# Projecting a part's groups at once and reading x1 four groups behind, in a two-layer graph kernel

## What is computed

```
W         = einsum('rb,bio->rio', w_comp, weight)             # 16 types from 8 bases
node_repr = segment_sum((x @ W[type])[src], dst) + h_bias
x1        = layernorm(x + node_repr)
deg       = maximum(segment_sum(1, dst), 1)
agg       = segment_sum(x1[src], dst)
out       = layernorm(x1 + x1 @ W_self + b_self + agg / deg @ W_neigh)
```

## Time and profile before

| | us |
|---|---|
| median of 3 runs | 3176.4 |
| fastest, slowest run | 3176.38, 3180.55 |
| profiled execution, span | 4143.4 |
| span less median | 967.0 |

### The profile page before, as it was taken

One profiled execution on the slowest core, in us unless ns is written; L12 is line 12 of the kernel. 1 busy time (PEld: TensorE's weight loads), 2 busy tenths in 40 slices (PEclk: granted clock), 3 DMA queues, 4 the chain that ended last, 5 costly groups with the idle time before them and its releaser, 6 DMA issues. The chain is left out here.

```text
span 4143.4 us, 36092 instructions
## 1 busy us (share of the span) xinstructions
PE 2142.2 (52%) x12511; PEld 2001.1 (48%) x12511; DVE 1431.9 (35%) x3693; ACT 332.1 (8%) x668; POOL 2392.4 (58%) x2524
## 2 busy tenths in 40 slices
PE   2455555555655555465555555567144444444445
PEld 1455445555555555455555555566143333333345
DVE  5242222122221222222221221222255657666635
ACT  1110000000000000000000000001000000000001
POOL 6645555555555555555556555565666666666663
PEclk7776666666666666666666665666555666666666
DMA  3832332233332332333333332332112222122222
GB/s 103 240 104 83 93 89 84 83 89 93 87 89 85 93 87 83 87 88 89 87 87 93 88 86 85 87 98 70 47 53 54 54 54 61 53 61 62 61 81 64
DMA packets 257427, 345.24 MB, mean 83 GB/s; under 512 B 47008, under 2 KB 189957, under 8 KB 257238
## 3 DMA queue, kind: packets, MB, share of 16 engines
q0 software_dynamic: 104400, 263.16, 22.7%
q1 hardware_dynamic: 127398, 66.86, 5.5%
q10 hardware_dynamic: 25440, 12.85, 1.0%
HBM read 311.14 MB, written 44.38 MB: 86 GB/s over the span
## 5 line engine op out<-in xcount | busy, mean ns | idle before, releaser
L1639 POOL DMA_INDIRECT rows<-x_x_rows,src_t x1501 | 1427.7, 951 | 1164.2 <-DMA x_x_rows<-xout 463.0
L2241 PE MATMUL zps<-acc,rows 128*128 128x168 f32 x3322 | 761.6, 363 | 570.6 <-issue 461.1
L2241 PEld LDWEIGHTS zps<-acc,rows 128*128 128x128 f32 x3322 | 611.5, 226 | 644.3 <-issue 598.7
L1666 POOL DMA_INDIRECT rows<-x_rows,picked_mem x691 | 655.9, 949 | 347.0 <-issue 196.1
L1887 DVE TENSOR_TENSOR acc<-acc,yps 128x63 f32 (+1 forms) x563 | 123.6, 220 | 1162.2 <-PE yps L2276 966.5
L2255 PEld LDWEIGHTS yps<-oh,rows 128*128 128x128 f32 x2058 | 336.6, 229 | 315.6 <-issue 315.4
L2255 PE MATMUL yps<-oh,rows 128*128 128x21 f32 x2058 | 313.6, 275 | 323.4 <-issue 321.5
L1865 DVE TENSOR_TENSOR acc<-oh,tps 128x1344 f32<-128x1344 f32 x208 | 323.3, 1554 | 141.7 <-remote 108.2
L2376 PE MATMUL zps<-acc,rows 128*128 128x128 f32 x1382 | 274.3, 356 | 121.9 <-issue 117.0
L2376 PEld LDWEIGHTS zps<-acc,rows 128*128 128x128 f32 x1382 | 244.9, 263 | 144.3 <-issue 144.2
L1718 ACT COPY acc<-zps 128x672 f32<-128x672 f32 x208 | 148.2, 714 | 1977.8 <-remote 1786.4
(11 more groups left out here) (315 smaller groups left out, 1882.0 us busy)
## 6 DMA issues: line engine op xcount, KB each, us to landing
rows<-x_x_rows,src_t POOLq DMA_INDIRECT x1501
acc<-in_edge_type_dram SPq DMA_DIRECT2D x207, 64.0 KB
x_x_rows<-zrow ACTq DMA_DIRECT2D x20, 576.0 KB, 3.3
x_x_rows<-in_x_dram SPq DMA_DIRECT2D x20, 576.0 KB
rows<-x_rows,picked_mem POOLq DMA_INDIRECT x691
x_rows<-xout SPq DMA_DIRECT2D x49, 128.0 KB
xin<-in_x_dram SPq DMA_DIRECT2D x48, 128.0 KB
out_dram<-xout SPq DMA_DIRECT2D x24, 256.0 KB
```

What stands on the lines that cost most here:

```text
L1639: gather = pool.indirect_dma_start(out=wide_rows[:, g % WIDE_SLOTS, c, :], out_offset=None, in_=table, in_offset=bass.IndirectOffsetOnAxis ...
L1666: pool.indirect_dma_start(out=rows[:, j % SLOTS, c, :], out_offset=None, in_=x1_rows[0:n_nodes, :], in_offset=bass.IndirectOffsetOnAxis(ap ...
L2241: last = nc.tensor.matmul(zwins[g % 2][:, c // HALF, c % HALF // 2], slot_rows(g, c), a[:, g % 4, c], start=(c % 2 == 0), stop=(c % 2 == 1 ...
```

## The change

The groups of a part are no longer projected in pairs. `project(r)` (line 2297 of the changed kernel) multiplies all 4 or 5 groups of a part at once, with 336 or 420 columns, into a PSUM bank of its own (`tps[1]`), between the two halves of the next group; the first and the last part are split in two runs. `zsb` has room for 5 groups. DVE adds the layer sums of all of the part's groups one after the other in that round (`add_sums`), and the early sums and degrees of each pair apart from them (`add_pair_windows`), from two banks that take turns. The part is staged one group after its last one and turned in the group after that. READABLE is 8, and a part is first read at half group 2 * done_at(k) + 8, which is group done_at(k) + 4: four whole groups, 32 gathers, lie between. SP waits for the pair adds before it stores degrees. The constants that follow from `front` change a little: 859 late columns instead of 852. The steps of the preamble that work out the same numbers for the data are adapted, and a few tiles lie elsewhere.

```diff
-READABLE = 9
+READABLE = 8
+RUN = 5
...
-        return per_group * (max(h - READABLE, 0) // 4 * 2 + 1)
+        return per_group * (max(h - READABLE, 2) // 2 - 1)
 
     def front(h):
         return 0 if h < 2 * PLAIN else min(FRONT, readable(h) // 17)
...
-        sums = first_layer(4 * DUOS * n_bases * SPAN)
-        zsb = sums.rearrange("p (u w b n) -> p u w b n", u=4, w=DUOS, b=n_bases)
+        sums = first_layer(RUN * DUOS * n_bases * SPAN)
...
+            runs = []
+            for k in range(all_parts):
+                g0, g1 = done_at(k - 1) if k else 0, done_at(k)
+                middle = [2] if k == 0 else [last_group] if k == last_part else []
+                bounds = [g0] + middle + [g1]
+                runs += [(r0, r1, k, r0 == g0) for r0, r1 in zip(bounds[:-1], bounds[1:])]
+            run_of = {g: r for r, (r0, r1, k, first) in enumerate(runs) for g in range(r0, r1)}
+            run_ends = {r1: r for r, (r0, r1, k, first) in enumerate(runs)}
+            assert len(run_of) == groups and all(r1 - r0 <= RUN for r0, r1, k, first in runs)
+
+            staged_at = {done_at(k): k for k in range(all_parts)}
+            turned_at = {done_at(k) + 1: k for k in range(all_parts)}
...
+            cleared_at = {done_at(k) + 3: k for k in range(all_parts)}
...
-            loops_at = {(1, 3, 7, 11)[k]: k for k in range(len(quads))}
+            loops_at = {(2, 3, 4, 8)[k]: k for k in range(len(quads))}
...
-            banks = [ybank[0], ybank[1], tps[1][:, :, :].rearrange("p t e -> p (t e)")]
...
+            ybank1 = tps[1][:, :, :].rearrange("p t e -> p (t e)")
+            windows = [y[:, 0:2 * 2 * DUOS * SPAN].rearrange("p (k w n) -> p k w n", k=2, w=2 * DUOS) for y in ybank]
+
+            def sums_col(g):
+                r0, r1, k, first = runs[run_of[g]]
+                return (g - (done_at(k - 1) if k else 0)) * DUOS * SPAN
...
                         if k < last_part:
+                            sp.wait_ge(pair_added, done_at(k))
                             store_degrees(stored1[s])
...
-                            after(act, w1.y_done, g // 2 - 1)
-                            nc.scalar.copy(zsb[:, g % 4].rearrange("p (h w) b n -> p h (w b n)", h=2),
+                            after(act, w1.y_done, run_of[g])
+                            nc.scalar.copy(zsb[:, kept_at(g)].rearrange("p (h w) b n -> p h (w b n)", h=2),
                                            zduos[g % 2]).then_inc(w1.z_copied, 1)
...
-                    def add_sums(g):
-
-                        first = 1 if narrow(g) else 0
+                    def starts_of(g):
                         _, starts = nc.values_load_multi_w_load_instructions(
                             base[0:1, g * DUOS:g * DUOS + duos_of(g)], engines=DVE_ONLY, min_val=0, max_val=n_nodes,
                             skip_runtime_bounds_check_because="clamped to the number of nodes, and acc is padded")
-                        dve.wait_ge(w1.y_done, products_before(g))
+                        return starts
+
+                    def add_pair_windows(g):
+
+                        first = 1 if narrow(g) else 0
+                        starts = starts_of(g)
+                        dve.wait_ge(deg_done, g // 2 + 1)
+                        after(dve, pair_added, g)
+                        for c in range(duos_of(g)):
+                            target = kinds3[:, 2 * first:3:2, bass.ds(starts[c], SPAN)]
+                            if c:
+                                dve.wait_ge(pair_step, g * (DUOS - 1) + c)
+                            add = nc.vector.tensor_tensor(target, target, windows_of(g)[:, first:2, c, :], ALU.add)
+                            add.then_inc(pair_step if c < duos_of(g) - 1 else pair_added, 1)
...
+                    def add_sums(g):
+
+                        starts = starts_of(g)
+                        dve.wait_ge(w1.y_done, run_of[g] + 1)
                         after(dve, w1.group_added, g)
                         for c in range(duos_of(g)):
-                            target = kinds3[:, first:3, bass.ds(starts[c], SPAN)]
+                            target = mem[:, bass.ds(starts[c] + SHIFT, SPAN)]
+                            y0 = sums_col(g) + c * SPAN
                             if c:
                                 dve.wait_ge(w1.rmw, g * (DUOS - 1) + c)
-                            add = nc.vector.tensor_tensor(target, target, windows_of(g)[:, first:3, c, :],
-                                                          ALU.add)
+                            add = nc.vector.tensor_tensor(target, target, ybank1[:, y0:y0 + SPAN], ALU.add)
...
-                        if g % 2 == 0 and 2 <= g < groups:
-                            add_sums(g - 2)
-                            add_sums(g - 1)
-                        if groups <= g < groups + 2:
-                            add_sums(g - 2)
+                        if g % 2 == 0 and 2 <= g <= groups:
+                            add_pair_windows(g - 2)
+                            add_pair_windows(g - 1)
+                        if g in run_ends:
+                            for e in range(*runs[run_ends[g]][0:2]):
+                                add_sums(e)
                         if g in out_at:
                             part_done(out_at[g])
...
+                            last = nc.tensor.transpose(tps[1][:, j, :], stage[:, j, :], ident[:, :])
...
-                                bank_free("pair", g // 2)
-                            if g == last_group:
-                                bank_free("single", g)
+                                after(pe, pair_added, g - 2)
...
-                    def project_pair(p):
-                        pe.wait_ge(w1.z_copied, 2 * p + 2)
-                        two = zsb[:, 2 * p % 4:2 * p % 4 + 2].rearrange("p u w b n -> p (u w) b n")
+                    def project(r):
+
+                        r0, r1, k, first = runs[r]
+                        pe.wait_ge(w1.z_copied, r1)
+                        if first:
+                            after(pe, n1.added, k)
+                        else:
+                            pe.wait_ge(w1.group_added, r0)
+                        if r == 1:
+                            pe.wait_ge(s_loopc, len(quads) - 1)
+                        if r == 2:
+                            pe.wait_ge(s_loopc, len(quads))
+                        duos = (r1 - r0) * DUOS if r1 < groups else (last_group - r0) * DUOS + duos_of(last_group)
+                        kept = zsb[:, 0:r1 - r0].rearrange("p u w b n -> p (u w) b n")
+                        y0 = sums_col(r0)
                         for b in range(n_bases):
-                            last = nc.tensor.matmul(windows[p][:, 1], wb[:, b, :], two[:, :, b, :],
+                            last = nc.tensor.matmul(ybank1[:, y0:y0 + duos * SPAN].rearrange("p (w n) -> p w n", n=SPAN),
+                                                    wb[:, b, :], kept[:, 0:duos, b, :],
                                                     start=(b == 0), stop=(b == n_bases - 1))
                         last.then_inc(w1.y_done, 1)
...
                     scale_by_relation(0)
-                    for g in range(groups - 2):
+                    for g in range(groups):
...
                         sum_half(g, 0)
                         early_half(g, 0)
+                        if g in run_ends:
+                            project(run_ends[g])
                         if g in turned_at:
                             turn_part(turned_at[g])
                         sum_half(g, 1)
                         early_half(g, 1)
                         if g % 2:
                             count_pair(g // 2)
-                            project_pair(g // 2)
                         if g in loops_at:
                             turn_loops(loops_at[g])
-
...
+                    project(run_ends[groups])
                     turn_part(last_part)
```

115 lines of the change are left out of this document (38 added, 77 removed).

## The result

The changed kernel takes 3222.7 us (median of 4 runs, 3211.5 to 3227.5) where the kernel before takes 3176.4 (4 runs, 3176.0 to 3180.6): ratio 1.0141, 95% interval 1.0128 to 1.0153. That is 46.4 us slower. The forecast was 3185.1; the range, 3120 to 3225, holds the result near its upper end, because it was drawn to take in rival B, the slower one.

The account below looks back on a forecast made before the run. POOL's gathers were taken to bound both phases, with x1 in time: 3176.4 us plus 8.7 for 7 more gathers, all other steps at nothing, gave 3185.1 us. Forecast's own range 3180 to 3190, overall 3120 to 3225.

Parts of the forecast that it names:

- rival B: Chain to x1 with PE at 1.2 GHz: projection takes 9.2 us, five-group parts wait, 3230 us; chance 0.12.
- The waits are a cost of recording, which the runs don't pay: POOL's waits in the earlier profile, 931.6 us of its 4143.4 us span, were taken as absent from the 3176.4 us runs.
- The pace derived: POOL's gathers: at most 1.242 us each fits the runs, 1% under the profile's pace.
- Step 1: READABLE and the reading rule: 7 more gathers at 1.242 us in POOL's late columns, +8.7 us.
- Step 2: Projection in one piece on PE: 5.0 us for four groups, ending 14.2 us after the part's last gather; nothing.
- Step 3: Adds apart on DVE: 300 us more work, covered by POOL; x1 there at 27, 30 or 33 us against 39.7; nothing.
- slack 13, 10 or 7: Time in us left between x1 in the table and its first reader, after 32 gathers (39.7 us); nothing waits.
- Step 4: New waits on PE, SP and ACT, such as PE about 2 us per part at `turn_part`: all at nothing.
- Step 5: Change of phases: the 16 held gathers (20 us) cover the last part's chain of some 16 us; nothing.
- Rival A: x1 waits are in the runs too and later reading shortens them: 3069 to 3145 us; chance 0.28.
- the prediction's own sign of being wrong: Runs slower by over 12 us would mean that a chain called covered isn't.

Follow-up runs that it names:

- experiment 1: The kernel before, profiled once more with no edit: a run of 4167.9 us with a span of 4166.4.
- experiments 7 and 8: 7: the change with READABLE 10, 3211.4 us, ratio 1.0101; 8: the change with the scaled operand ahead of the layer sums and READABLE 12, 3204.4 us, ratio 1.009.
- experiment 8: The change with edge types' marks and scaled operand ahead of the layer sums and READABLE 12, against the kernel before: 3204.4 us, ratio 1.009.

## Why the prediction was right or wrong

- **"The waits are a cost of recording, which the runs don't pay"** (what bounds the kernel): wrong, and experiment 1 shows it. The use made of it held all the same, and that was luck: on a faster machine POOL's gathers bound both phases with few waits in the three kernels profiled there, and by the estimate above in the kernel before. The pace derived, at most 1.242, was 1% low, since from the start of the last gather to the end it is 20.1 to 20.7 us there, and not the 53.4 of the earlier trace rows: measured 1.252.
- **Step 1, 7 gathers, +8.7**: right. 698 at line 1671, 8.8 us; and the accounts of experiments 7 and 8 close with further gathers at that price.
- **Step 2, the projection at once**: the price at full clock was near (four groups take 4.77 us where the clock is full throughout, 5.0 said), but the sum took that clock for all. The 592 recorded matmuls of 336 columns take 238.7 us together, 6.5 us per part of four groups, between the 5.0 of the sum and the 9.2 of rival B: by the trace's records of the clock the projections ran at the full one for 46% of their time. (The 580 ns in the page's row is no price, since neighbouring matmuls overlap in it.) For part 12 the projection ended 21.8 us after the last gather instead of 15.4: PE began it 4.9 us late, and it took 7.7 us instead of 6.2.
- **Step 3, adds apart, "slack 13, 10 or 7"**: this is where the prediction failed. The trains were right (five groups 7.3 us, 6.9 said; 177 ns an add, 176 in the earlier trace rows). From one group's adds to the next DVE had 1.28 + 0.36 us before and has 1.14 + 0.41 and 1.19 + 0.38 now, 1.48 more, where the step gave 1.45. So the separation lengthens DVE's work, as the step said against the rule on breaking up instructions in the Trainium skill, page "Perfetto Trace Analysis", section "Optimizing Scalar/DVE Operations"; no row here shows work completed sooner by it. But the chain was summed as a straight line of its own steps. For a part of five groups it came to 33 us and took 43.9: 6.4 of the 10.9 had come by the end of the projection, and 3.8 came between the last layer sum and the part's end on DVE: 5.1 in the sum, for an operand and the pair adds of two groups, and 8.9 in the trace (613.9 to 622.9), as DVE had done those and still waited for the turn.
- **Step 4, "PE stands at `turn_part` about 2 us ... All at nothing"**: the 2 us are right (112.7 us in 38 places, 2.3 per part), the nothing is not. The step asked what is queued behind PE's wait and not what is queued behind DVE's. DVE's wait for the projection (14.56 us at part 12) had the operand of PE's next `scale_by_relation` behind it. It could be read from the two lists of instructions: the train stands ahead of line 1870, and with done_at % 4 == 1 the operand is wanted one group later.
- **Step 5, the change of phases, "nothing"**: 9.2 us over the pace. The last part's chain, from the end of the first phase's last gather to the first gather that waits for it, took 29.4 us where the step had some 16; in experiment 8, without the two waits shown there, 22.1.
- **Rival B**, PE at the lower clock, 3230 with a chance of 0.12, was nearest to what happened: the clock was at 1.2 GHz in the stretch before the late part. But it had no wait of PE for an operand in it, and that it came within 8 us is partly luck, as the places were others: not twelve parts of five groups by their length, but those with done_at % 4 == 1, and 23 us rather than 45, with the rest at the change of phases and group 21. The clock of 0.50 in the earlier trace rows had spoken for it, and its weight was set too low.
- **Rival A**, that x1 waits would fall: it holds on the slower chips for the reading rule alone (0.97), and not even there for the whole change (1.039).
- The chance of slower, 0.48, was the largest of the three, but the sum was 37.6 us too low, and the prediction's own sign of being wrong came true: over 12 us slower, "then a chain I called covered isn't". The forecast's own range of 3180 to 3190 failed as well; the overall range holds the result only by its share of B.

## What to carry to other kernels

When work is gathered into one longer wait, go through the list of the engine that waits and ask what stands behind the wait, and which other engine needs that next; an operand for the next step belongs ahead of a wait for the last one. A slack summed along one chain holds only if every engine in it is free when the chain comes by, so sum it at the engine's lower clock and with its arrears. And compare a profile's span with its own run's time before explaining the gap: a span far over the listed runs can come from another machine.

## What the runs showed of the hardware

- **The same kernel takes 3176 us on some chips and 4144 to 4204 on others**, each within 1.1% of itself. Each chip has one set of runs on record, so whether it is the chip or something else about those runs isn't shown. Gathers are the same there (947 to 951 ns, and 0.30 to the next), and so are single matmuls (eight recorded ones of 168 columns take 1.30 us at the higher clock and 2.6 at the lower on both). What differs is PE between matmuls: 1536 us of "issue" for the kernel before, and 1429 for the change there, against 5 for the change on a faster chip. I don't know the cause. The mean granted clock of the kernel before is 0.658 there and 0.680 on the faster chip, which looks too little for a difference of 30%.
- **A verdict on such a kernel can turn with the chip**: the change costs 1.4% on one and 3.9% on another, and later reading, which costs its gathers on a faster chip, gains up to 7.7% on a slower one, together with the scaling put first.
- After a pause of PE of 2.46 us its clock fell to 1.2 GHz, and it stayed there for some 37 us, although PE was busy for 37 of the 40 us around them.
